# A causal mask added by TensorE instead of VectorE, shorter router fillers, and VectorE copies of the reciprocals in the last attention

## The reference

```python
def attention(x, c_attn_w, c_proj_w):
    B, T, C = x.shape                      # 1, 256, 192
    H, D = (N_HEAD, C // N_HEAD)           # 12 heads of 16
    qkv = x @ c_attn_w.T
    q, k, v = jnp.split(qkv, 3, axis=-1)
    ...
    scores = jnp.einsum('bhqd,bhkd->bhqk', q, k) * (1.0 / math.sqrt(D))
    causal = jnp.tril(jnp.ones((T, T), dtype=bool))
    scores = jnp.where(causal, scores, -jnp.inf)
    att = jax.nn.softmax(scores, axis=-1)
    y = jnp.einsum('bhqk,bhkd->bhqd', att, v)
    ...
    return y @ c_proj_w.T
```

## Time and profile before

| | us |
|---|---|
| median of 3 runs | 401.25 |
| lowest and highest of the 3 | 400.78, 403.18 |
| the profiled execution, its own time | 403.34 |
| its span, first to last instruction | 401.5 |
| the last attention from its first score product to its last projection, in the span | 231.9 to 253.7 |
| PE busy in the span | 376.3 |
| DVE, ACT, POOL busy in the span | 247.5, 175.0, 108.8 |

### The profile page before, as it was taken

One profiled execution on the slowest core, in us unless ns is written; L12 is line 12 of the kernel. 1 busy time (PEld: TensorE's weight loads), 2 busy tenths in 40 slices (PEclk: granted clock), 3 DMA queues, 4 the chain that ended last, 5 costly groups with the idle time before them and its releaser, 6 DMA issues.

```text
span 401.5 us, 9820 instructions
## 1 busy us (share of the span) xinstructions
PE 376.3 (94%) x3806; PEld 248.0 (62%) x3806; DVE 247.5 (62%) x662; ACT 175.0 (44%) x441; POOL 108.8 (27%) x166
## 2 busy tenths in 40 slices
PE   8999999999999999999999988989999999999996
PEld 6776645566777645666676755746666655655444
DVE  3776488765476587764576587442246577547773
ACT  1488234441278253540397178322143445243351
POOL 5821356310001365310001301320024442026330
PEclk9999899999999999999999999899999999999999
DMA  6399940071399700091499500327990301991000
GB/s 189 80 308 300 365 91 2 2 203 36 115 244 381 221 2 3 2 212 27 147 231 336 191 1 2 118 61 252 312 307 18 91 2 53 284 309 66 2 2 20
DMA packets 28680, 56.09 MB, mean 140 GB/s; under 512 B 5260, under 2 KB 15963, under 8 KB 28635
## 3 DMA queue, kind: packets, MB, share of 16 engines
q1 hardware_dynamic: 26978, 53.88, 45.8%
q10 hardware_dynamic: 1657, 1.60, 1.2%
HBM read 53.25 MB, written 2.22 MB: 138 GB/s over the span
## 4 chain that ended last, share of the span: by engine, by line
PE 68%; DVE 11%; issue 9%; ACT 6%; DVEq 2%; DMA 1%; POOL 1%; SPq 1%; POOLq 0%; ACTq 0%
PE bank L1419 11%; PE bank L1351 8%; PE bank L1358 5%; PE bank L1009 5%; PE bank L1378 4%; ACT sw L821 4%; PE bank L1135 4%; PE bank L1162 3%; PE bank L1447 3%; PE bank L1048 3%; PE bank L1178 2%; PE bank L1434 2%; PE bank L1144 2%; PE bank L1253 2%; PE bank L1286 2%
## 5 line engine op out<-in xcount | busy, mean ns | idle before, releaser
L821 ACT ACTIVATE sw<-bank,nmax 128x256 f32<-128x256 f32 (+1 forms) x96 | 43.3, 478 | 11.7 <-DVE nmax L1650 7.4
L906 ACT ACTIVATE hT<-bank 128x384 f32<-128x384 f32 x34 | 16.4, 489 | 67.5 <-PE bank L1378 67.5
L1009 PE MATMUL bank<-warm 128*128 128x256 f32 x158 | 44.5, 424 | 1.2 <-DVE warm L1951 1.2
L1836 DVE COPY sw<-rw 128x1344 f32 (+1 forms) x32 | 31.2, 985 | 9.7 <-PE bank L1366 6.0
L646 POOL COPY sw<-rinv 128x64 f32<-128x64 f32 x48 | 9.7, 238 | 96.2 <-DVE rinv L1663 93.0
L1009 PEld LDWEIGHTS bank<-warm 128*128 128x128 f32 x158 | 31.7, 212 | 5.5 <-DVE warm L1951 1.2
L1419 PE MATMUL bank<-sw,hT 128*32 128x192 f32 x630 | 32.6, 330 | 0.0
L710 POOL COPY sw<-rw 128x1344 f32 (+1 forms) x12 | 21.7, 1812 | 37.5 <-PE bank L1366 24.2
L1135 PE MATMUL bank<-kT,qT 64*128 64x256 f32 (+1 forms) x192 | 24.1, 380 | 4.2 <-ACT sw L821 3.0
L1162 PE MATMUL bank<-consts,sw 128*128 128x128 f32 x180 | 25.5, 279 | 2.4 <-issue 1.1
L1419 PE MATMUL bank<-rw,hT 128*32 128x192 f32 (+1 forms) x432 | 25.9, 330 | 1.4 <-ACT hT L906 1.4
(11 more groups left out here) (234 smaller groups left out, 739.9 us busy)
## 6 DMA issues: line engine op xcount, KB each, us to landing
rw<-in_M_w_dram SPq DMA_DIRECT2D x16, 1152.0 KB, 16.3
rw<-in_M_w_dram SPq DMA_DIRECT2D x16, 768.0 KB, 7.0
rw<-in_M_w_dram SPq DMA_DIRECT2D x36, 192.0 KB, 8.0
rw<-in_M_w_dram SPq DMA_DIRECT2D x8, 576.0 KB, 9.1
wqkv<-in_A_wqkv_dram SPq DMA_DIRECT2D x4, 432.0 KB, 4.1
rw<-in_M_w_dram SPq DMA_DIRECT2D x16, 96.0 KB, 5.1
wproj<-in_A_wproj_dram SPq DMA_DIRECT2D x4, 288.0 KB, 5.0
bqkv<-in_A_bqkv_dram SPq DMA_DIRECT2D x3, 288.0 KB, 4.5
```

The source lines that it names most:

```text
L821: act.activation(probs[:, p % 2, h, t, 0:keys_of(n, t)], scores_bank(p, h)[:, t, 0:keys_of(n, t)], ACT.Exp, bias=nmax[:, p % 2, h, t:t + 1 ...
L1009: pe.matmul(bank[b][:, 0:T], warm[:, 0:P], warm[:, :], start=True, stop=True)
L1836: dve.tensor_copy(sw1[:, 1 + i, 0:n1], rw1[:, bass.ds(ids[4 * i + d], 1), 0:n1].rearrange("p a n -> p (a n)")).then_inc(w1c_dve, 1)
```

## The change

Three edits. First, in the last attention the mask is no longer added by VectorE: after each score product of a head and a query tile, PE adds a product of the bf16 identity (`counting[:, 2]`, 128 x 128) with a bf16 copy of the mask (`later_keys`, 128 x 128, written once by GpSimd at the start) into the diagonal block of the same scores. Second, `WARM_ROUTER` goes from 4 to 2. Third, in the last attention the copies of the broadcast reciprocals from PSUM to SBUF go from ScalarE's queue to VectorE's, each directly in front of the multiplication that uses it.

```diff
-WARM_LN, WARM_ROUTER = 3, 4
+WARM_LN, WARM_ROUTER = 3, 2
...
+        later_keys = sb("later_keys", [P, P], BF16)
...
+            pool.tensor_copy(later_keys[:, :], consts[:, CONST["causal"]]).then_inc(counting_ready, 1)
             pool.tensor_copy(counting[:, 0], consts[:, CONST["earlier"]]).then_inc(counting_ready, 1)
...
                 turned(1)
                 exps(3)
-                scales(0)
+                if n < 3:
+                    scales(0)
...
                     for t in range(TT):
                         for h in range(2):
                             ins = pe.matmul(scores_bank(p, h)[:, t, 0:keys_of(n, t)], qT[head_rows(h), p, t * P:(t + 1) * P],
-                                            kT[head_rows(h), p, 0:keys_of(n, t)], start=True, stop=True)
+                                            kT[head_rows(h), p, 0:keys_of(n, t)], start=True, stop=n < 3, skip_group_check=n == 3)
+                            if n == 3:
+
+                                ins = pe.matmul(scores_bank(p, h)[:, t, t * P:(t + 1) * P], counting[:, 2], later_keys[:, :],
+                                                start=False, stop=True, skip_group_check=True)
                             if t == TT - 1:
                                 ins.then_inc(s_psum, 1)
...
-                    pe.wait_ge(counting_ready, 3)
+                    pe.wait_ge(counting_ready, 4)
...
                         if n == 3:
-
-                            mask = consts[:, CONST["causal"]].unsqueeze(1).broadcast_to([P, TT, P])
-                            own_keys = bank[B_S[p % 2][h]][:, 0:TT * (T - P) + TT * P].rearrange("p (a k) -> p a k", k=P)[:, 0:4:3]
-                            then(dve.tensor_tensor(own_keys, own_keys, mask, ALU.add))
-                            settle()
                             for t in range(TT):
...
                 def scaled(g):
 
+                    if n == 3:
+                        dve.wait_ge(scale_psum, GROUPS * n + g + 1)
+                        dve.wait_ge(o_ready, GROUPS * n + g - 1)
+                        dve.tensor_copy(rscale[:, (GROUPS * n + g) % 2, :], scales_bank(g)).then_inc(scale_ready, 1)
                     dve.wait_ge(scale_ready, GROUPS * n + g + 1)
                     dve.wait_ge(o_psum, GROUPS * n + g + 1)
```

More of the change, by code:

```diff
@@ L853, in attn @@
                 exps(5, 1)
-                scales(1)
+                if n < 3:
+                    scales(1)
                 turned(5)
@@ L860, in attn @@
                         act.dma_start(rw1[b * CR:b * CR + BIAS_PARTS, :, BIAS_AT].bitcast(BF16), b1_row(0, b, 0, E)).then_inc(b1_row_in, 16)
-                scales(2)
+                if n < 3:
+                    scales(2)
             def moe(m):
```

## The result

The changed kernel takes 413.0 us, median of four runs (409.54 to 420.12), against 401.19 for the kernel before (400.78 to 403.18): a ratio of 1.0238, 95% interval 1.0189 to 1.0288. It is slower, as forecast, but takes about 7 us more than the 406.0 that was predicted, outside the range of 401.3 to 408.9. The run of 420.12, at a mean granted clock of 0.955, is left out of the ratio.

What follows compares the result with a forecast made beforehand. No engine was taken as full in the last attention: VectorE paces its start, PE its end. From 403.34, +6.3 for masks and -3.0 for fillers give 406.6; 406.0 was taken, range 404 to 408, 8 in 10 within 401.3 to 408.9.

Steps and rivals of the forecast that it cites:

- The price of a mask: Last attention: weight loads, tile changes and heads no longer side by side make a pair 2.76 us in place of 0.86.
- rival 1: Last attention: masks hide in PE's waits and VectorE's relief decides, 397.8 to 398.0 us; chance 0.10.
- rival 2: Last attention: PE loads weights ahead across the change of tile size, about 3 us less, 403 us; chance 0.12.
- The sum for the stage: Last attention: six pairs add 11.3 us on PE, 5.0 hidden in its waits, leaving +6.3 us.
- VectorE's relief: Last attention: twelve masks fewer, 5.5 us of VectorE's work; worth nothing with PE the bound, otherwise 0.46 + 1.6 us.
- The copies: Last attention: three reciprocal copies moved from ScalarE to VectorE sum to 0, at worst +0.8 us; -0.4 if ScalarE bound.
- rival 3: Last attention: the clock falls there too, one or two falls at up to 1.5 us, 407.5 to 409 us; chance 0.08.
- PE full: Last attention: PE is full, and shorter fillers give back a part, 404 to 408 us; chance 0.70.
- the fillers' term: Routers of experts 0, 1, 2: shorter fillers gain -1.2, -0.2, -1.7, sum -3.0 us; -0.8 where the clock doesn't fall.

Runs made afterwards that it cites:

- half the rows: Changed kernel with each mask product cut to the 64 rows of its head's score product (half the mask missing): 401.4 us, 0.998 of the kernel before.
- 4 columns: Changed kernel with each mask product cut to 4 of its 128 columns, all 128 rows kept: 417.0 us, 1.036 of the kernel before.
- Masks last: Changed kernel with a pair's four mask products behind its four score products: 401.4 us; 399.9 us with only a bank's first score product marked as start.
- the mask alone: Kernel before with only the mask as a product behind each score product, four fillers and ScalarE's copies kept: 411.3 us, 1.019 of the kernel before.
- two halves, four fillers: Kernel before with each mask as two 64-row products behind its score product, four fillers and ScalarE's copies kept: 398.7 us, 0.989 of the kernel before.
- masks last with four fillers: Kernel before with a pair's four mask products behind its four score products, four fillers and ScalarE's copies kept: 399.2 us, 0.992 of the kernel before.
- copies alone: Kernel before with only the last attention's reciprocal copies moved to VectorE, its mask and four fillers kept: 403.1 us, 0.998 of the kernel before.
- four-fold masks: Changed kernel with each mask product issued four times in a row, each adding a fraction of the mask: 414.1 us, 1.026 of the kernel before.
- the fillers alone: Kernel before with two fillers per router stage in place of four, nothing else: 403.0 us, 0.998 of the kernel before.

## Why the prediction was wrong in size

**The price of a mask held.** Forecast 0.58 and 0.80 us for a score with its mask and 2.76 for a pair; measured 0.58, 0.79 and 2.74. The causes held too, each in a row of the changed kernel at full clock:

```profile
241.98 0.27 PE L1140 MATMUL bank<-kT,qT 64*128 64x128 f32 x1
242.18 0.23 PE L1144 MATMUL bank<-later_keys,counting 128*128 128x128 bf16 x1
```

The second pass starts 0.22 behind the first (241.76), so 0.11 for weights that weren't loaded ahead; the mask starts 0.20 behind that, 0.09 more than the pass streams; the next score, at 242.34, starts 0.16 behind the mask, which leaves 0.09 over the 0.07 of its stream. The Trainium skill, TensorEngine Tiling (Array Packing), section Tiling Modes, was weighed in the prediction for saying that a change of the tiling mode drains TensorE. These rows agree, 0.09 us each way.

The experiments say the same. Without the change of tile the pair falls to 0.93 (half the rows), without most of the stream it stays at 2.52 (4 columns). Masks last keeps 12 of the 48 changes and takes 1.19. Rivals 1 and 2 are out for this order of the products; the mechanism of rival 1 comes true in the other order.

**The sum for the stage held at full clock.** Forecast +6.3 us, with 5.0 of the 11.3 hidden in TensorE's waits (six times 1.9 is 11.4, so 6.4 by the text's own numbers). By the estimate above it is 28.6 - 22.0 = +6.6, and 0.4 of that is the wait at the stage's end that the mask alone doesn't have.

**VectorE's relief held.** It was called worthless while TensorE is the bound and 0.46 + 1.6 us where it isn't. Where it isn't (masks last and two halves, four fillers) the stage is 2.1 shorter. Only the sum is shown to agree: in masks last with four fillers ScalarE's waits for the maxima add up to 3.0 us, against 4.0 before.

**The copies** were put at 0, at worst +0.8. The first, covered by the maxima's wait for TensorE in the forecast, costs 0.3 where VectorE sets the pace (copies alone). The third is over before the last values are, as forecast, but in the changed kernel the multiplication behind it starts 0.3 late and the stage is 0.4 longer, for a reason not found; the time of the kernel with the copies alone doesn't show a loss.

**The step that failed is rival 3 and its counterpart in the fillers: the clock.** The forecast let TensorE run at full clock through the last attention and gave a fall there a chance of 0.08, at 1.5 us each. The profiled fall costs 2.9 us, what the text has for two: the second pair takes 4.18 in place of 2.74 (233.82 to 238.00, +1.4), and the queries' transposes and fillers from 238.00 to 240.99 take 2.99, where they take 1.52 at full clock in the kernel with four-fold masks (+1.5). So the price was right and the chance was not.

It was no rare case. The profile of the mask alone has the same fall, and the mean clocks of all runs point to it: with two fillers 0.975 for the change against 0.983 to 0.989 for the kernels whose profiled stage is at full clock, with four fillers 0.987 for the mask alone against 0.994 to 0.997. The 6.8 us of the profile take off 0.008. In which stage the runs that weren't profiled lost their clock isn't on record.

The argument that the runs fit stood in the text of the rival (TensorE streams a smaller part of the time) and was given too little weight against "PE full"; whether the half of the rows that it also names has a part in it wasn't tried. Busy was read as working: in the 4-column version TensorE's rows fill the stage and the clock is at half for most of it.

**The second half of that step is the fillers' term, -3.0.** Forecast -1.2, -0.2 and -1.7 at experts 0, 1 and 2 (-3.1 when added). Measured at the start of the gathering -1.6, 0.0 and -1.7. But what follows then runs at half clock: +0.6 behind experts 0 and +2.0 behind experts 2. Another 0.2 is lost inside attention 2, at full clock, for a reason that wasn't looked for. That leaves -1.0, +0.2 and +0.3. The prediction foresaw the loss at experts 0 and left out the larger one at experts 2. What came out (about -0.6 in this profile, and -0.9 for the fillers alone) is by chance near the -0.8 that the text has for a clock that doesn't fall.

Together: 403.34 + 6.6 + 2.9 - 0.6 = 412.2, and 412.43 was measured. Of the 5.8 us between that and the 406.6 that the prediction has from the same base, the fall in the stage makes 2.9 and the fillers 2.4. (The medians miss by 1.2 more: 406.0 was taken 0.6 below 406.6, and 413.0 lies 0.6 above the profiled execution.)

**What stays open.** The profiles show that the clock falls in the stage when masks and scores take turns, for longer with less streamed between two changes of tile and not at all with four times as much. Each of the last two is one profile, and the same kernel's mean clock differs from run to run (0.979 to 0.988 for the four-fold masks), so the order is likely but not shown beyond that; at which point the clock falls they don't tell. Nor was it tried why two fillers lower the clock over a whole run (0.986 against 0.992) though they save time at an equal clock.

## What to carry to other kernels

Before work moves to TensorE, ask what lies next to it in the queue: a mask of about 0.05 us of stream made its score 0.5 us longer (a pair of 2.74 in place of 0.76, for four masks) because it stood between products of another tile size, and the same 24 products behind their scores cost 0.33 us a pair, which fitted into TensorE's waits and let VectorE's relief through. Put products of one size together, or cut the new one to the size around it. And an engine whose rows leave no gap can still lose its clock; before and after are best compared at an equal mean granted clock, and fillers that nothing waits for any more may still be paying for the work behind them.

## What the runs showed that was not expected

Less work on TensorE made the kernel slower: masks of 4 columns 417.0 us, of 128 columns 413.0, and four times 128 columns 414.1, with 20.4, 6.8 and 0 us of the profiled stage at half clock. At an equal mean clock (0.979) the 4 columns are no slower: 412.9, against 412.4 and 413.6 for the change. And 48 products of 64 rows took 1.04 us a pair where 24 of 128 rows took 2.74.
